# Two window-attention layers: 64x64 pieces of the TensorE array for the scores, windows taken in pairs with half of the heads each

## The chip, the cores and the metric

One core of a Trainium2 chip (trn2). The metric is the device time of the whole kernel in microseconds (us), from one launch. Everything is float32 where not said otherwise.

## What is computed

A batch of 16 images of 96 channels and 16x16 pixels goes through four residual layers, `x = x + layer(group_norm(x))`. Layers 0 and 1 are window attention: each image has four windows of 8x8 = 64 tokens, and 12 heads. Layer 2 is a quantized depthwise and pointwise convolution, layer 3 a spiking linear attention; the change does not touch them. Cut to what matters:

```python
# layer 0: head size 8, a bias per head, biases on q, k, v
qkv = xw @ qkv_w.T + qkv_b                       # xw: windows (64 tokens) x 96 channels
attn = einsum('bhnd,bhmd->bhnm', q * 8**-0.5, k) + rpb_table[rel_index]   # per head
out = softmax(attn) @ v ; out = out @ proj_w.T + proj_b
# layer 1: head size 32, image rolled by 4, one bias for all heads, masks in three of the four windows
dots = einsum('bhwid,bhwjd->bhwij', q, k) * 32**-0.5 + pos_emb[...] (+ UD_MASK, LR_MASK)
out = softmax(dots) @ v ; out = out @ w_out + b_out
```

## The kernel before

After some 120 us of loads and preparation the two attention layers run one after the other, each as 16 images ("samples"), software-pipelined by hand over five engines. Within a sample the unit of work is a *step*, four to a sample; before the change a step is one window with all 12 heads. Its scores lie in a tile `probs[w]` of 128 partitions (two heads x 64 queries) x 6 x 64 keys. Each step goes through this chain, and each engine runs its own queue strictly in the order written:

- PE, `pe_scores` (L749): six matmuls of 128x128x128 into one of the two banks `ps_scores[w % 2]`. The stationary operand is q of a window, masked so that of 128 columns each holds one head's 64 tokens (`q0` has 6 masked copies a sample, `q1` has 2 for each of 3 groups); the moving operand is k of the window and of the next (128 columns, of which the first 64 are wanted; the next group overwrites the rest). The zeros in k (rows of the other half `u`) and in q make the 128-deep contraction right. A bank is free once the vector engine has taken it (`biased`).
- DVE, `dve_scores`: add the bias from PSUM to `probs[w]` (L913) and row maximum (L916). POOL, `pool_shift` (L947): subtract it. ACT, `act_exp` (L804). DVE, `dve_sum` (L921, L923): row sum and reciprocal. POOL, `pool_scale` (L952).
- PE, `pe_transpose` (L757): three transposes into `ps_probsT`. ACT, `act_probsT` (L809): copy to SBUF. PE, `pe_values` (L770 in layer 1, L780 in layer 0): six matmuls with zero-padded v into `ps_heads`. ACT, `act_heads` (L814 four times a sample in layer 1, L817 once a sample in layer 0). Then per sample `pe_out` (L796, L798), `act_out` (L823) and `pool_residual` (L964).

Ahead of this, q, k and v of the next samples are made: DVE `dve_norm` (L938) writes the normalized image, PE `pe_qkv` (L720 for q and k, L728 for v) fills the two banks `ps_qkv` in turn, and each use of a bank is emptied by the engine that `qkv_plan` names, in so many instructions (`evac_q`, `evac_k`, `evac_v`: L836 or L842, L853 or L854, L866 or L873). PE may fill a bank again only when all of them are done.

The order is fixed by `pe_sample`, `act_sample`, `dve_sample` and `pool_sample`: in step w, DVE does the scores of w+2, then the sums of w+1, then the evacuations that `evacs_at[w]` lists; ACT does its evacuations first, then the exponential of w+2, then the copy of the transposes of w; PE, before the change, does half of the scores of w+3, the transposes of w, the other half, the values of w-1, then the q, k, v uses that `uses_at[w]` lists. So the scores of a step stand on PE more than a step ahead of the moment DVE wants them.

Of the kernel before, what the change touches and what calls it, by code (L numbers as in the profile page):

```python
# [25 lines left out]
ALU = mybir.AluOpType  # L26
# [4 lines left out]
T = SIDE * SIDE  # L31
# [13 lines left out]

CONSTS = {}
_at = 0
for _name, _n in (("ident", 128), ("qmask0", 6), ("qmask1", 2), ("group_mean", C), ("ones", 128),
                  ("head_blocks", C), ("masks", 4 * WT), ("rows", 2), ("minus_half", 1), ("perm", 4 * 128)):
    CONSTS[_name] = (_at, _at + _n)  # L50
    _at += _n
# [3 lines left out]
def constants():  # L55
# [10 lines left out]
    put("qmask0", (p[:, None] % 64 // HD0 == np.arange(NP * NH)) * np.float32(HD0 ** -0.5))  # L66
    put("qmask1", (p[:, None] // HD1 % 2 == np.arange(2)) * np.float32(HD1 ** -0.5))
# [7 lines left out]
    m = np.zeros((2, WT, NW, WT), bool)  # L75
    for w in range(NW):
        m[:, :, w] |= (ud & (w // 2 == 1)) | (lr & (w % 2 == 1))
    put("masks", m.reshape(128, NW * WT) * np.float32(NEG))


    perm = np.zeros((WT, NW, NH, WT))
    for w in range(NW):
        src = (tok // WIN + w // 2 * 4) % WIN * WIN + (tok % WIN + w % 2 * 4) % WIN
        perm[WT - 1 - src, w, :, tok] = 1
    put("perm", perm.reshape(WT, NW * 128), WT)
# [5 lines left out]
class Attention:  # L91


    def __init__(self, n, hd):
        self.n, self.hd = n, hd
        self.wide = hd == HD1
        self.slots = 2 if self.wide else NP * NH
# [8 lines left out]
        self.evacs_at = [[(1, 2, 0, 4)], [(1, 3, 0, 4)], [(1, 4, 0, 4)], [(2, 0, 0, 4), (2, 1, 0, 4)]] if self.wide else \  # L106
            [[(1, 0, 3, 6), (1, 1, 0, 2)], [], [(1, 2, 0, 4)], [(2, 0, 0, 3)]]


class AttentionSems:  # L110


    def __init__(self, sem, n):
# [5 lines left out]
        self.scores_ready = sem(f"l{n}_scores_ready")  # L119
        self.biased = sem(f"l{n}_biased")  # L120
# [15 lines left out]
def build(nc, a, out):  # L136

    ctx = ExitStack()
    with ctx:
# [30 lines left out]
        b0_q = sb("b0_q", [128, NP * NH])  # L170
        b0_v = sb("b0_v", [128, 2 * C])
# [8 lines left out]
        bias0 = sb("bias0", [128, NP * NU, WT])  # L180
# [5 lines left out]
        bias1 = sb("bias1", [128, NW, WT])  # L186
# [36 lines left out]
        q0 = [sb(f"q0_{i}", [128, NW, NP * NH, WT]) for i in range(2)]  # L223
        k0 = [sb(f"k0_{i}", [128, NU, T + WT]) for i in range(2)]

        v0 = [sb(f"v0_{i}", [128, NW * NP, NH, NH * NU * HD0]) for i in range(2)]
        q1 = [sb(f"q1_{i}", [128, 3, NW, 2, WT]) for i in range(2)]
        k1 = [sb(f"k1_{i}", [128, NU, NP, T + WT]) for i in range(2)]
        v1 = [sb(f"v1_{i}", [128, NW * NP, NH, NU * HD1]) for i in range(2)]
        probs = [sb(f"probs{i}", [128, NP * NU, WT]) for i in range(4)]  # L230
        row_max = [sb(f"row_max{i}", [128, NP * NU]) for i in range(4)]
        probsT = [sb(f"probsT{i}", [128, NP * 128]) for i in range(2)]
# [46 lines left out]
        def wait(eng, s, v):  # L279

            if not (isinstance(v, int) and v <= 0):
                eng.wait_ge(s, v)
# [59 lines left out]
        def first_loads():  # L342
# [8 lines left out]
            for k in range(2):  # L351
                yield b0_v[:, k * C:(k + 1) * C], a["L0_conv_qkv_b"][2 * C:3 * C].unsqueeze(0).broadcast_to([128, C])

            for h in range(NH):
                for u in range(NU):
                    yield (p0_raw[:, :].rearrange("o (p h u d) -> o h u p d", p=NP, h=NH, u=NU)[:, h, u],
                           a["L0_conv_proj_w"].rearrange("o (p u h d) -> o h u p d", p=NP, h=NH, u=NU)[:, h, u])
            yield p0_b[:, :], a["L0_conv_proj_b"].unsqueeze(1)

        def late_loads():  # L360
            yield w1[0:C, :], a["L1_conv_w_qkv"]

            for h in range(NH):
                for u in range(NU):
                    yield (p1[(h * NU + u) * HD1:(h * NU + u + 1) * HD1, :, :],
                           a["L1_conv_w_out"].rearrange("(p u h d) c -> h u d p c", p=NP, u=NU, h=NH)[h, u])
# [11 lines left out]
        def _(act):  # L378
# [4 lines left out]
            for dst, src in late_loads():  # L383
# [16 lines left out]
                        *(t[:, :, :] for t in k0),  # L400

# [1124 lines left out]
```

## Time and profile before

| | us |
|---|---|
| median of 3 runs | 680.67 |
| lowest, highest of them | 677.33, 831.42 |
| profiled execution: span from first to last instruction | 674.8 |
| median of the runs over that span | 5.9 |
| PE busy, DVE busy, ACT busy, POOL busy in the span | 522.9, 479.1, 319.7, 304.6 |

The span is that of one profiled execution; the time of a run also holds what lies around the first and the last instruction. Of the span, some 115 us are loads and preparation, about 190 us layer 0 (to 308 us), 250 us layer 1 (to 557 us) and 118 us layers 2 and 3. A matmul of float32 appears in the trace as two records (a transpose as one), so twelve records are six matmuls. The duration of a single record is longer than the distance between two, since they overlap; the chain of waits gives the distance.

### The profile page before, as it was taken

The page shows a single profiled execution, that of the slowest core. Times are in us where ns is not written, and L with a number is a line of the kernel's source. Part 1 is how long each engine was busy: PE and PEld are TensorE (multiplying, and loading weights), DVE is VectorE, ACT ScalarE, POOL GpSimd, SP SyncE. Part 2 cuts the span into 40 slices and gives each one's busy share as a digit, 9 for nine tenths or more (in the row PEclk, how much of TensorE's full clock was granted, in tenths as well). Part 3 has the DMA queues.
Part 4 walks back from the last instruction along what each step waited for, and adds up shares of the span by engine and source line. Part 5 has one row for each costly group of instructions (what it writes and reads, how often), then busy time and mean ns, then how long its engine had stood idle before and what let it go on. Part 6 is the DMA issues. An engine that isn't in the chain of part 4 may idle for free.

```text
span 674.8 us, 13829 instructions
## 1 busy us (share of the span) xinstructions
PE 522.9 (77%) x4459; PEld 420.9 (62%) x4459; DVE 479.1 (71%) x1237; ACT 319.7 (47%) x746; POOL 304.6 (45%) x482
## 2 busy tenths in 40 slices
PE   0000087689999999986999999999999998867664
PEld 0000086678888888874788888888888772323432
DVE  0000357699999999985788888788888748966784
ACT  0000000447575756644466666666666553226673
POOL 9000001267676666673365545555555553340322
PEclk9999999999999999999899999999999999987786
DMA  1111300000000000000000000000000000000001
GB/s 58 47 54 47 89 9 0 1 1 2 1 0 0 0 0 0 0 1 1 1 1 3 1 0 0 0 0 0 0 0 0 0 1 1 0 1 0 24 23 47
DMA packets 9808, 7.04 MB, mean 10 GB/s; under 512 B 6371, under 2 KB 9443, under 8 KB 9667
## 3 DMA queue, kind: packets, MB, share of 16 engines
q1 hardware_dynamic: 3954, 5.01, 2.4%
q10 hardware_dynamic: 5826, 1.67, 1.2%
q8 instruction: 15, 0.25, 0.2%
q14 instruction: 13, 0.11, 0.1%
HBM read 5.11 MB, written 1.57 MB: 10 GB/s over the span
## 4 chain that ended last, share of the span: by engine, by line
PE 49%; DVE 19%; SPq 11%; issue 7%; POOL 7%; ACT 4%; DVEq 1%; DMA 1%; POOLq 0%; ACTq 0%
PE bank L749 16%; SPq L327 11%; PE bank L720 9%; PE bank L757 5%; PE bank L770 4%; PE bank L796 3%; DVE conv L1172 3%; DVE probs L913 3%; DVE xn L938 3%; PE bank L728 3%; DVE row_max L916 3%; PE bank L1253 3%; POOL probs L952 3%; PE bank L557 2%; POOL probs L947 2%
## 5 line engine op out<-in xcount | busy, mean ns | idle before, releaser
L749 PE MATMUL bank<-k,q 128*128 128x128 f32 x1536 | 216.1, 278 | 8.2 <-issue 4.5
L749 PEld LDWEIGHTS bank<-k,q 128*128 128x128 f32 x1536 | 199.3, 193 | 22.7 <-issue 7.2
L947 POOL TENSOR_TENSOR probs<-probs,row_max 128x384 f32<-128x384 f32 x128 | 106.0, 828 | 181.2 <-DVE row_max L916 180.5
L804 ACT ACTIVATE probs<-probs 128x384 f32<-128x384 f32 x128 | 67.1, 524 | 115.1 <-POOL probs L947 113.9
L952 POOL TENSOR_TENSOR probs<-probs,inv_sum 128x384 f32<-128x384 f32 x128 | 106.1, 829 | 3.7 <-DVE inv_sum L923 3.7
L913 DVE TENSOR_TENSOR probs<-bank,bias 128x384 f32<-128x384 f32 x128 | 71.1, 555 | 35.8 <-PE bank L749 33.4
L916 DVE TENSOR_REDUCE row_max<-probs 128x6 f32<-128x384 f32 x128 | 70.8, 553 | 4.4
L539 PE MATMUL bank<-pos,cst 64*128 64x16 f32 x32 | 7.0, 371 | 86.1 <-DMA pos<-in_L_conv_pos_emb 86.1
L921 DVE TENSOR_REDUCE row_sum<-probs 128x6 f32<-128x384 f32 x128 | 69.5, 543 | 2.2 <-ACT probs L804 2.1
L757 PE MATMUL bank<-cst,probs 128*128 128x128 f32 x384 | 64.3, 276 | 7.2 <-POOL probs L952 5.6
L809 ACT COPY probsT<-bank 128x384 f32<-128x384 f32 x128 | 59.9, 468 | 2.9 <-PE bank L757 1.7
L842 ACT ACTIVATE q<-bank,b_q,cst 128x256 f32<-128x256 f32 x96 | 47.0, 564 | 29.4 <-PE bank L720 29.4
L539 PEld LDWEIGHTS bank<-pos,cst 64*128 64x128 f32 x32 | 6.9, 329 | 86.0 <-issue 86.0
L433 DVE CAST table_parts<-table 113x12 bf16<-113x12 f32 (+1 forms) x2 | 0.3, 175 | 78.1 <-DMA table<-in_L_conv_rpb_table 78.1
L720 PE MATMUL bank<-xn,w 128*128 128x256 f32 x192 | 51.5, 406 | 3.9 <-DVE v L866 3.2
L757 PEld LDWEIGHTS bank<-cst,probs 128*128 128x128 f32 x384 | 45.0, 141 | 12.3 <-POOL probs L952 12.1
L618 POOL TENSOR_SCALAR gn_veps<-gn_var 96x8 f32<-96x8 f32 x8 | 2.7, 340 | 104.2 <-DVE gn_var L612 104.2
L938 DVE TENSOR_SCALAR xn<-x,gn_mean,gn_rstd 96x32 f32 (+3 forms) x160 | 45.2, 347 | 0.1
L1454 ACT ACT_TABLE_LOAD x1 | 1.3, 1283 | 92.1 <-issue 92.1
L964 POOL TENSOR_TENSOR x<-y_attn,x 96x32 f32 (+3 forms) x160 | 42.5, 290 | 4.6 <-ACT y_attn L823 4.6
L720 PEld LDWEIGHTS bank<-xn,w 128*128 128x128 f32 x192 | 34.9, 195 | 11.1 <-issue 3.8
L836 ACT ACTIVATE q<-bank,cst 128x256 f32<-128x256 f32 x64 | 26.8, 470 | 23.9 <-PE bank L720 23.9
(144 smaller groups left out, 854.8 us busy)
## 6 DMA issues: line engine op xcount, KB each, us to landing
rel_bc<-in_L_conv_rel_index SPq DMA_DIRECT2D x1, 1808.0 KB
x<-in_x SPq DMA_DIRECT2D x4, 384.0 KB, 32.6
out_dram<-y_out SPq DMA_DIRECT2D x8, 192.0 KB, 2.1
cst<-in_consts ACTq DMA_DIRECT2D x1, 613.5 KB
w<-in_L_conv_w_qkv ACTq DMA_DIRECT2D x1, 432.0 KB, 3.9
p<-in_L_conv_w_out ACTq DMA_DIRECT2D x4, 36.0 KB, 3.3
b_qk<-in_L_conv_qkv_b ACTq DMA_DIRECT2D x8, 0.1 KB, 5.4
pos<-in_L_conv_pos_emb SPq DMA_DIRECT2D x8, 2.0 KB
```

The costliest lines, as they stand in the source:

```text
L327: sp.dma_start(x[:, i * n * T:(i + 1) * n * T].rearrange("c (b t) -> c b t", t=T), a["x"][i * n:(i + 1) * n].rearrange("b c h w -> c b (h ...
L720: last = nc.tensor.matmul(o[:, half * T:(half + 1) * T], w[:, col:col + 128], xn[par][:, :, :], start=True, stop=True)
L749: last = nc.tensor.matmul(ps_scores[w % 2][:, g * WT:(g + 2) * WT], q, k, start=True, stop=True)
L757: last = nc.tensor.transpose(ps_probsT[w % 2][:, p * 128:(p + 1) * 128], probs[w][:, 2 * p:2 * p + 2, :], ident)
L804: nc.scalar.activation(probs[w][:, :, :], probs[w][:, :, :], ACT.Exp).then_inc(L.s.exped, 1)
L809: nc.scalar.copy(probsT[w % 2][:, :], ps_probsT[w % 2][:, 0:NP * 128]).then_inc(L.s.probsT_sb, 1)
L913: nc.vector.tensor_tensor(probs[w][:, :, :], ps_scores[w % 2][:, 0:NP * NU * WT].rearrange("p (g k) -> p g k", k=WT), b, ALU.add).then_inc ...
L916: nc.vector.tensor_reduce(row_max[w][:, :], probs[w][:, :, :], AX.X, ALU.max).then_inc(L.s.maxed, 1)
L921: nc.vector.tensor_reduce(row_sum[w][:, :], probs[w][:, :, :], AX.X, ALU.add).then_inc(L.s.summed, 1)
L938: nc.vector.tensor_scalar(of_tokens(tokens), of_image(image(x_of(s))), gn_mean[:, bass.ds(s * 1, 1)], gn_rstd[:, bass.ds(s * 1, 1)], ALU.s ...
L947: nc.gpsimd.tensor_tensor(probs[w][:, :, :], probs[w][:, :, :], by_row(row_max[w]), ALU.subtract).then_inc(L.s.shifted, 1)
L952: nc.gpsimd.tensor_tensor(probs[w][:, :, :], probs[w][:, :, :], by_row(inv_sum[w]), ALU.mult).then_inc(L.s.scaled, 1)
```

## The change

A step is now a pair of windows (2j and 2j+1, index c) with half of the heads (index u), so there are still four steps a sample and each `probs[w]` still has 128 partitions (two windows x 64 queries) x 6 heads x 64 keys. The scores of both halves u of a pair are made by one call: twelve matmuls with a contraction of 64 rows (`rows = u*64..`), a stationary q of 64 columns and a moving k of 128 columns (two heads, of which each copy of k is masked to one). Rows u and output partitions c put each on one of four 64x64 quarters of the array, in the order p, c, u; half u goes to bank u. q is no longer masked by head (layer 1: one copy; layer 0: three copies, masked by group), k is, in two copies, by window. All evacuations of q and k are now ACT's. In layer 1 one copy of the heads serves a pair. The biases of v in layer 0 move to the copy of the heads. Lines of the new file: scores L749, transposes L758, values L771 and L783, exp L807, copy of the transposes L812, heads L817 (layer 1), q L838 or L844, k L857 or L861, v L881, norm L947, q and k matmuls L719, v matmuls L727, out L799 and L801.

Core of the diff:

```diff
-            return [("qk", 0, "act", 4), ("qk", 1, "dve", 4), ("qk", 2, "act", 4),
+            return [("qk", 0, "act", 3), ("qk", 1, "act", 3), ("qk", 2, "act", 3),
                     ("v", 0, "dve", 4), ("v", 1, "act", 4)]
-        return [("q", 0, "act", L.slots), ("k", 0, "dve", 2), ("v", 0, "dve", 4)]
+        return [("q", 0, "act", 3), ("k", 0, "act", 2), ("v", 0, "dve", 4)]
...
-        self.evacs_at = [[(1, 2, 0, 4)], [(1, 3, 0, 4)], [(1, 4, 0, 4)], [(2, 0, 0, 4), (2, 1, 0, 4)]] if self.wide else \
-            [[(1, 0, 3, 6), (1, 1, 0, 2)], [], [(1, 2, 0, 4)], [(2, 0, 0, 3)]]
+        self.evacs_at = [[(1, 2, 0, 3)], [(1, 3, 0, 4)], [(1, 4, 0, 4)], [(2, 0, 0, 3), (2, 1, 0, 3)]] if self.wide else \
+            [[(1, 1, 0, 2)], [], [(1, 2, 0, 4)], [(2, 0, 0, 3)]]
...
-    def pe_scores(pe, L, s, w, half):
-        if half == 0:
-            if w == 0:
-                for i in range(L.qk_uses):
-                    evacuated(pe, L, s, i)
-            wait(pe, L.s.biased, win_count(s, w - 2))
-        keys = slice(w * WT, (w + 2) * WT)
-        for g in range(half * NP, (half + 1) * NP):
-            p, u = g // NU, g % NU
-            if L.wide:
-                q, k = q1[par][:, p, w, :, :], k1[par][:, u, p, keys]
-            else:
-                q, k = q0[par][:, w, p * NH:(p + 1) * NH, :], k0[par][:, u, keys]
-            last = nc.tensor.matmul(ps_scores[w % 2][:, g * WT:(g + 2) * WT], q, k, start=True, stop=True)
+    def pe_scores(pe, L, s, j):
+        if j == 0:
+            for i in range(L.qk_uses):
+                evacuated(pe, L, s, i)
+        free = wait(pe, L.s.biased, win_count(s, 2 * j - 1))
+        for p in range(NP):
+            for c in range(2):
+                w = 2 * j + c
+                for u in range(NU):
+                    rows = slice(u * 64, (u + 1) * 64)
+                    q = (q1 if L.wide else q0)[par][rows, p, w * WT:(w + 1) * WT]
+                    k = k1[par][rows, p, w, :, :] if L.wide else k0[par][rows, w, :, :]
+                    one = nc.tensor.matmul(ps_scores[u][c * WT:(c + 1) * WT, p * 128:(p + 1) * 128], q, k,
+                                           start=True, stop=True)
+                    if p == NP - 1 and c == 1:
+                        one.then_inc(L.s.scores_ready, 1)
...
     def pe_sample(pe, L, s, prev, nxt, nxt2):
-        for w in range(NW):
-            ahead = w < 1 or nxt
-            if ahead:
-                pe_scores(pe, L, *at(s, w + 3), 0)
-            pe_transpose(pe, L, s, w)
-            if ahead:
-                pe_scores(pe, L, *at(s, w + 3), 1)
-            if w >= 1 or prev:
-                pe_values(pe, L, *at(s, w - 1))
-            if w == 1 and prev:
-                pe_out(pe, L, moved(s, -1))
-            q = uses(L, s, w, nxt, nxt2)
-            if q[2]:
-                pe_qkv(pe, L, *q)
+        for j in range(2):
+            if j == 0 or nxt:
+                pe_scores(pe, L, *pair_at(s, j + 1))
+            for u in range(NU):
+                w = 2 * j + u
+                pe_transpose(pe, L, s, w)
+                if u == 0 and (j or prev):
+                    pe_values(pe, L, *pair_at(s, j - 1))
+                q = uses(L, s, w, nxt, nxt2)
+                if q[2]:
+                    pe_qkv(pe, L, *q)
+            if j == 0 and prev:
+                pe_out(pe, L, moved(s, -1))
```

The values of a pair are twelve matmuls in one call (`pe_values(L, s, j)`, layer 0 in the order c, u, p, layer 1 in p, c, u), after the first transposes of the next pair. Evacuation of q and k, in short (q of layer 1 before: two masked copies; k before: once for each u and 64 rows, now once for each h and 128 rows, with the mask as scale):

```diff
-            src, dst = by_window(ps_qkv[b][:, 0:T]), q1[par][:, j, :, slot, :]
+            src, dst = ps_qkv[b][:, 0:T], q1[par][:, j, :]
-        rows = slice(u * 64, u * 64 + 64)
-        src = ps_qkv[b][rows, T:2 * T]
+        src = by_window(ps_qkv[b][:, T:2 * T])
+        scale = cst[:, lo:lo + 1]
```

In the preparation: the masked copies of k need no zeroed buffers; the constant table shrinks from 1227 to 842 columns; the position matmuls (L539, now L534) have 64 instead of 128 stationary columns and write windows 2j and 2j+1 to the two halves of the partitions; the bias of layer 0 is reduced once for 64 rows and then copied to the other 64 (one more DVE copy of 64x768); on ACT's DMA queue two broadcast loads of 128x96 become one of 96x1, four strided loads of `p0_raw` become one, and four of `p1` become one. On SP's queue nothing changes.

PE in layer 1, second half of a sample in the straight code ahead of the loop (steps 2 and 3). Before:

```order
L749 MATMUL bank<-k_0,q_0 128x128 x3
L757 MATMUL bank<-cst,probs 128x128 x3
L749 MATMUL bank<-k_0,q_0 128x128 x3
L770 MATMUL bank<-probsT,v_1 64x64 x6
L720 MATMUL bank<-xn,w 128x256 x4
L749 MATMUL bank<-k_0,q_0 128x128 x3
L757 MATMUL bank<-cst,probs 128x128 x3
L749 MATMUL bank<-k_0,q_0 128x128 x3
L770 MATMUL bank<-probsT,v_1 64x64 x6
L720 MATMUL bank<-xn,w 128x256 x2
```

The same half now (the first row holds the scores of the next sample's first pair; the scores of its second pair come after the last row):

```order
L749 MATMUL bank<-k_0,q_0 64x128 x12
L758 MATMUL bank<-cst,probs 128x128 x3
L771 MATMUL bank<-probsT,v_1 64x64 x12
L719 MATMUL bank<-xn,w 128x256 x4
L758 MATMUL bank<-cst,probs 128x128 x3
L719 MATMUL bank<-xn,w 128x256 x2
```

The scores that stood around every step's transposes now stand once a pair, ahead of them, and the two q and k matmuls of the third use come right before the next scores instead of after scores that DVE will want a step later.

ACT in layer 1, the same two steps. Before (evacuations of v; then of q and k of one use):

```order
L866 COPY v_0<-bank 64x6x32 x4
L804 ACTIVATE probs<-probs 128x384
L809 COPY probsT<-bank 128x384
L814 COPY heads_1<-bank 128x3x64
L836 ACTIVATE q_1<-bank,cst 128x4x64 x2
L853 COPY k_1<-bank 64x256 x2
L804 ACTIVATE probs<-probs 128x384
L809 COPY probsT<-bank 128x384
```

And now:

```order
L881 COPY v_0<-bank 64x6x32 x4
L807 ACTIVATE probs<-probs 128x384
L812 COPY probsT<-bank 128x384
L817 COPY heads_1<-bank 128x3x128
L838 ACTIVATE q_1<-bank 128x256
L857 ACTIVATE k_1<-bank,cst 128x4x64 x2
L838 ACTIVATE q_1<-bank 128x256
L857 ACTIVATE k_1<-bank,cst 128x4x64 x2
L807 ACTIVATE probs<-probs 128x384
L812 COPY probsT<-bank 128x384
```

The second use's q and k have come over from DVE and stand between the evacuation that PE waits for and the exponential that DVE waits for.

## Rows read from the trace of the kernel before

**Rows 1.** The page: busy time by engine, and the granted TensorE clock in 40 slices.

```profile
PE 522.9 (77%) x4459; PEld 420.9 (62%) x4459; DVE 479.1 (71%) x1237; ACT 319.7 (47%) x746; POOL 304.6 (45%) x482
...
PEclk9999999999999999999899999999999999987786
```

**Rows 2.** Windows: stretch, its length, busy by engine (instructions), clock, DMA share, GB/s.

```profile
115.00:120.00 5.00, 2.05 (x4) 1.18 (x4) 1.94 (x6) 2.56 (x6) 0.00 (x0) 1.00 0.01 2
...
170.00:210.00 40.00, 39.37 (x433) 34.66 (x431) 36.99 (x98) 24.86 (x57) 27.37 (x44) 1.00 0.00 0
...
395.00:435.00 40.00, 40.00 (x368) 34.98 (x368) 33.30 (x87) 26.02 (x68) 21.47 (x40) 1.00 0.00 0
```

**Rows 3.** Chain of waits in layer 1, 410 to 440 us: start, length, what.

```profile
by line: PE bank L749 35.7%; PE bank L720 22.0%; PE bank L770 15.0%; PE bank L728 9.9%; PE bank L796 9.8%; PE bank L757 8.7%
...
424.41 0.50 PE bank L770 x12
...
426.83 0.67 PE bank L749 x6
...
428.99 1.06 PE bank L720 x4
...
439.00 0.50 PE bank L770 x12
```

**Rows 4.** Timeline of DVE in layer 1: start, length, line, tiles, count.

```profile
428.67 0.56 DVE L913 TENSOR_TENSOR probs<-bank,bias 128x384 f32<-128x384 f32 x1
...
430.98 1.63 DVE L938 TENSOR_SCALAR xn<-x,gn_mean,gn_rstd 96x64 f32 x6
...
432.53 0.54 DVE L913 TENSOR_TENSOR probs<-bank,bias 128x384 f32<-128x384 f32 x1
...
435.86 0.56 DVE L913 TENSOR_TENSOR probs<-bank,bias 128x384 f32<-128x384 f32 x1
```

**Rows 5.** Timeline of the same stretch of layer 1, ACT and POOL.

```profile
430.09 0.84 ACT L836 ACTIVATE q<-bank,cst 128x256 f32<-128x256 f32 x2 [0.73 <-PE bank L720]
...
433.74 0.83 POOL L947 TENSOR_TENSOR probs<-probs,row_max 128x384 f32<-128x384 f32 x1 [2.23 <-DVE row_max L916]
...
434.60 0.52 ACT L804 ACTIVATE probs<-probs 128x384 f32<-128x384 f32 x1 [1.76 <-POOL probs L947]
...
435.03 0.46 ACT L809 COPY probsT<-bank 128x384 f32<-128x384 f32 x1
...
435.39 0.32 ACT L814 COPY heads<-bank 128x192 f32<-128x192 f32 x1
...
437.09 0.83 POOL L947 TENSOR_TENSOR probs<-probs,row_max 128x384 f32<-128x384 f32 x1 [1.74 <-DVE row_max L916]
```

**Rows 6.** Timeline of DVE in layer 0.

```profile
269.54 0.56 DVE L913 TENSOR_TENSOR probs<-bank,bias 128x384 f32<-128x384 f32 x1
...
271.36 0.56 DVE L913 TENSOR_TENSOR probs<-bank,bias 128x384 f32<-128x384 f32 x1
...
276.35 0.56 DVE L913 TENSOR_TENSOR probs<-bank,bias 128x384 f32<-128x384 f32 x1 [0.19 <-PE bank L749]
...
278.21 1.00 DVE L854 TENSOR_SCALAR k<-bank,b_qk 64x256 f32<-64x256 f32 x2
279.25 0.42 DVE L586 BATCH_NORM_STATS2 stats<-x  x1
...
280.58 0.56 DVE L913 TENSOR_TENSOR probs<-bank,bias 128x384 f32<-128x384 f32 x1
```

**Rows 7.** Chain of waits in layer 0: a step's values.

```profile
273.65 0.37 PE bank L780 x12
```

**Rows 8.** Chain of waits at the start of the kernel.

```profile
78.56 7.37 DMA pos<-in_L_conv_pos_emb
...
86.07 6.98 PE bank L539 x32
...
120.33 2.94 PE bank L749 x12
```

More of the change, by code:

```diff
@@ L361, in late_loads @@
             yield w1[0:C, :], a["L1_conv_w_qkv"]
[L363 to L366, printed above, removed]
+            yield p1[:, :, :], a["L1_conv_w_out"].rearrange("(p r) c -> r p c", p=NP)
             yield p1_b[:, :], a["L1_conv_b_out"].unsqueeze(1)
@@ L473, in bias_banks @@
                     n = min(BIAS_KEYS, WT - k0_)
-                    for h in range(NH):
-                        src = bank[2 + i][0:WT, 0:n * 3 * HEADS] \
-                            .rearrange("q (k part g h) -> q h g k part", k=n, part=3, h=NH)[:, h]
-                        step(nc.vector.tensor_reduce(bias0[h * WT:(h + 1) * WT, :, k0_:k0_ + n], src, AX.X, ALU.add))
+                    src = bank[2 + i][0:WT, 0:n * 3 * HEADS].rearrange("q (k part g) -> q g k part", k=n, part=3)
+                    step(nc.vector.tensor_reduce(bias0[0:WT, :, k0_:k0_ + n], src, AX.X, ALU.add))
             bias_banks(0, 2)
@@ L768, in pe_values @@
                 for p in range(NP):
-                    for h in range(NH):
-                        last = nc.tensor.matmul(ps_heads[h * WT:(h + 1) * WT, p * WT:(p + 1) * WT],
-                                                v1[parity(s)][:, w * NP + p, h, :], pT[:, p * 128 + h * WT:p * 128 + (h + 1) * WT],
-                                                start=True, stop=True)
+                    for c in range(2):
+                        for u in range(NU):
+                            last = nc.tensor.matmul(ps_heads[u * WT:(u + 1) * WT, p * 128 + c * WT:p * 128 + (c + 1) * WT],
+                                                    v1[par][:, 2 * j + c, p * NU + u, :],
+                                                    probsT[2 * j + u][:, p * 128 + c * WT:p * 128 + (c + 1) * WT],
+                                                    start=True, stop=True)
@@ new lines, in evac_v @@
+                dst = v1[par][rows, 2 * j + c, :, h * HD1:(h + 1) * HD1]
+            else:
+                src = ps_qkv[b][src_rows, 0:2 * C].rearrange("k (g u h d) -> k h g u d", u=NU, h=NH, d=HD0)[:, h]
+                n = 2 * NP
+                lo = h * HD0
+                step = NU * NU * NH * HD0
+                dst = v0[par][rows, c * n:(c + 1) * n, :, :].rearrange("k g u e -> k g (u e)")
+                dst = bass.AP(tensor=dst.tensor, offset=dst.offset + lo,
+                              ap=[dst.ap[0], [step, n], [NU * NH * HD0 + NH * HD0, NU], [1, HD0]])
@@ L875, in evacuate @@
+            return nc.scalar.copy(dst, src) if eng == "act" else nc.vector.tensor_copy(dst, src)
         def evacuate(eng, who, L, s, i, first=0, end=99):
```

195 lines of the change are left out of this document (97 added, 98 removed).

## Prediction, made before the changed kernel had run

> **What bounds the kernel now.** I read the page first. No engine is busy over 77% of the span [rows 1], but that is a mean over stages, so I read the windows of the two attention layers next. In layer 1 PE is busy 40.00 us of 40, in layer 0 39.37, and DVE 36.99 [rows 2]. Then the chain of waits. In layer 1 it stands on PE alone, 35.7% of it on the scores (L749), and one sample is 439.00 - 424.41 = 14.59 us [rows 3]. Eight groups of six score records at 0.67 are 5.36 us of these: 0.111 us a record of 128 columns. Last the timelines. In layer 0 a sample is 280.58 - 269.54 = 11.04 us [rows 6], and DVE idles only 0.19 us in it ahead of a step that waited for scores. So layer 1 is PE's, and layer 0 is DVE's with PE close behind. The loads and the preparation are a chain of their own [rows 8]; layers 2 and 3 don't change.
>
> **The scores.** There are as many score records as before, 48 a sample, but each uses a quarter of the array. What 24 of them (one pair) take, call it D, decides much. No row shows a matmul on half of the rows. From above: one after the other at 0.111 is D = 2.67. From below: four at a time without loss is 0.67. The nearest rows are the values, which already use a part of the columns each: twelve records in 0.50 us in layer 1 [rows 3], 0.042 each with the changes of shape around them, and twelve in 0.37 in layer 0 [rows 7], 0.031 each. Such records are of 64 columns and would take about 0.055 alone, so pieces of the array do work side by side, and 0.031 to 0.042 looks like what a record costs at least. 24 x 0.031 to 24 x 0.042 is 0.74 to 1.0; I take D = 0.9. The change of shape between matmuls is in the 0.042. The Trainium skill (TensorEngine Tiling, Array Packing, Key Properties) says that changing the tiling mode drains the engine, which would speak against more kinds of shapes in one queue. But the values changed it already, four times in and out a sample; now values and scores do so twice each, and the count is the same. The skill (TensorE: Matmul & The Clock Gate, Part 3, Packing small matmuls) gives tiles that run together the time of one plus 4 ns for each further one; by that three groups of four would be 3 x 0.235 = 0.70, an estimate from its rule, and the result some 3 us lower.
>
> **Layer 0.** DVE loses the two evacuations of k: 278.21 to 279.25, 1.04 us [rows 6]. The evacuations of v stay four, and all else on DVE keeps its size. ACT has 5 evacuations of 128x256 in place of 6 and 24.86 us of 40 busy [rows 2], so it covers k. Without k and the wait of 0.19 the sample is 9.81. What is late next? The scores of a pair may start when the second of the pair before has been taken: 0.56 us into its step. DVE wants them one step later, 271.36 - 269.54 = 1.82. 0.56 + 0.9 and two hops of 0.05 are 1.56: they fit, by 0.26. Once a sample PE comes to them a little late, after the out matmul, for which I put 0.1. So 9.9, a gain of 1.1, 14 times: 15.4 us.
>
> **Layer 1.** By sums it looks splendid: PE 14.59 - 5.36 + 1.8 = 11.0, DVE about 10.9 (two steps of 1.82 and the two stretches of the next sentences), ACT under 10. But the order closes a loop. PE does the third q/k use at the end of a sample; it needs the bank that ACT empties in step 3, and behind this use in PE's queue stand the scores that DVE wants at once. Before, those had been made in the step ahead. Once around: ACT empties the first use, 3 at 0.84/2 [rows 5] = 1.26; PE the third use 1.06 [rows 3]; scores 0.9; DVE step 0 with statistics and the norm, 428.67 to 432.53 = 3.86; step 1 with v, to 435.86 = 3.33 [rows 4]; from the start of step 2 to POOL's shift, 437.09 - 435.86 = 1.23; from shift to exponential 434.60 - 433.74 = 0.86; exponential, copy of the transposes and heads on ACT 0.43 + 0.36 + 0.36 [rows 5], and ACT is at the first use again. With two hops 13.75 us. That is the new period, with no engine busy over 80% of it. The gain is 0.84 x 14 = 11.8 us. It is bounded by 0 and by 14 x 3.5 = 49 (if the loop didn't close, DVE's 10.9 and some hops). If D grows, this loop grows by the same.
>
> **Ends of the layers.** In the last two samples of each layer no q, k, v are made; a step was PE's: 1.33 + 0.33 (three transposes at 0.111) and 0.37 or 0.50, so 2.04 and 2.17, and is DVE's 1.82 now. 8 x 0.22 + 8 x 0.35 is 4.6; I take 4.
>
> **Start.** PE's position matmuls stand on the chain with 6.98 us for 32 records [rows 8], 0.22 each, twice what a record of 128 stationary columns takes in the loops [rows 3]. With 64 columns I take half: 3.4 us less (0 to 3.5), since what follows waits for them. The position data land last on SP's queue, whose own loads don't change; the constants are 30% smaller and seven DMAs fewer go through the other queue beside it. That shares the engines that move them, so the position data may land earlier: I take 2 us (0 to 8, the latter a tenth of the 86). The one reduction less for each bias bank pays for the copy of the bias. The first scores took 2.94 us for twelve records [rows 8], at half pace; DVE can start a pair sooner, and the second window of it at once. ACT's last evacuation ahead of it comes some 0.4 sooner in layer 0 and a little later in layer 1. Together 4 us for both layers.
>
> **The sum.** 15.4 + 11.8 + 4 + 3.4 + 2 + 4 = 40.6 us. The span of 674.8 becomes 634.2. The median of the runs lay 5.9 above that span, which gives 640.
>
> **Rivals.** (1) *The quarters don't run side by side.* For: only pieces of columns are shown to do so, and here all need weights of their own. D = 2.67. In layer 0 DVE then waits at each second step, 0.56 + 2.67 + 0.1 - 1.82 = 1.51, twice a sample: 9.81 + 3.02 = 12.8, 1.8 more than before, 25 us. Layer 1: 13.75 + 1.77 = 15.5, 13 us more. Ends: 7 more; start 6 less. 680.7 + 39 = 720 us, slower. It decides from D = 1.9 on; below that the change wins. (2) *Only two at a time*, D = 1.33: layer 0 waits 0.17 twice, gains 0.9 (12 us), layer 1 0.41 (6), ends 3, start 8: 652 us. (3) *The clock.* PE falls from 98% busy in layer 0 to about 70%, and in the last four slices of the kernel the granted clock is 0.6 to 0.8 [rows 1]. Against: in a stretch with 2.05 of 5 us busy it was 1.00 [rows 2], and the gaps here are under a microsecond. At 1.2 in place of 2.4 GHz for half of the time, layer 1's loop would gain back 1.0 of its 0.84, layer 0's scores about 1 us a sample: about 670 us, no change that a measurement of this kernel can tell. (4) *Layer 1's loop doesn't close*, because ACT gets to the first use sooner than I have it, or PE's third use is ready earlier: each microsecond is 14. With half of it gone 620, with all of it 603 us.
>
> **How the numbers follow.** The forecast (632 to 648) has 0.58, rival 2 0.15, rival 4 to 622 and below 0.09, rival 3 and other small losses that leave nothing 0.11, rival 1 0.07. I count 2% (13.6 us) as what a measurement of this kernel can tell from no change. Faster: 0.58 + 0.15 + 0.09 and a little of the third, 0.84. Same 0.09, slower 0.07. The range takes in the forecast, the upper half of rival 4 and rival 2 with a clock or wait that costs 10 us more: 620 to 664.
>
> **What would show it.** The changed profile should have 24 score records of a pair (L749) in about 0.9 us; a layer 0 sample of 9.9 us with DVE nearly full; a layer 1 sample of 13.75 us in which DVE idles once a sample, ahead of step 0, for about 2.9 us with PE named, while PE itself idles ahead of L719 for ACT's k. The position matmuls should take 3.5 us. Score groups of 1.3 us or more, DVE waits ahead of every second step in layer 0, or a granted clock under 1 in the loops would prove it wrong; so would a layer 1 sample under 13 us with no wait of DVE for PE.

## The result, and the profile after

The changed kernel takes 655.54 us (median of 4 runs, 654.75 to 656.62) against 679.00 for the kernel before in the same session (4 runs, 675.88 to 831.42). The ratio is 0.969, with a 95% interval of 0.965 to 0.973: 3% faster. The run of 831.42 was a slow one, and the ratio compares fast runs alone. The forecast was 640 with a range of 620 to 664: the sign and the range hold, and of the gain of 40 us little more than half came, 23.5. The profiled span went from 674.8 to 653.0.

The page of the changed kernel, busy time and the granted clock:

```profile
PE 411.4 (63%) x4459; PEld 270.3 (41%) x4459; DVE 444.5 (68%) x1138; ACT 305.2 (47%) x714; POOL 299.2 (46%) x478
...
PEclk9999999959999999976899999999999989977786
```

PE lost 111.5 us of work [rows 1]; the records of L749 alone fell from 216.1 to 61.1 us. No engine is over 68% now. And the line of the clock has two dents that the one of before lacks: a 5 about 140 us in, the first samples of layer 0, and 7, 6, 8 about 290 us in, the end of layer 0. Stretches of the changed kernel, as in [rows 2]: the first samples of layer 0, its loop, its end, and the loop of layer 1:

```profile
130.00:170.00 40.00, 28.92 (x396) 19.95 (x389) 34.70 (x93) 21.90 (x50) 26.86 (x41) 0.79 0.01 2
...
210.00:250.00 40.00, 27.10 (x471) 18.61 (x469) 37.06 (x97) 25.34 (x58) 28.69 (x47) 1.00 0.00 0
...
280.00:285.00 5.00, 2.25 (x13) 1.55 (x17) 2.66 (x7) 2.15 (x5) 4.19 (x6) 0.82 0.00 0
...
290.00:295.00 5.00, 3.89 (x53) 2.95 (x54) 4.39 (x11) 2.12 (x5) 3.85 (x7) 0.50 0.00 2
295.00:300.00 5.00, 4.16 (x38) 2.49 (x39) 3.29 (x10) 2.25 (x6) 3.47 (x7) 0.50 0.02 5
...
390.00:430.00 40.00, 32.48 (x369) 22.30 (x370) 29.57 (x78) 26.36 (x72) 22.78 (x42) 1.00 0.00 0
```

Before, the stretch from 130 to 170 us ran at full clock:

```profile
130.00:170.00 40.00, 36.08 (x383) 31.63 (x382) 36.77 (x99) 22.80 (x52) 25.25 (x37) 1.00 0.01 2
```

Layer 0's loop is still DVE's (37.06 of 40). In layer 1 nothing is full. To see where the 21.8 us of span come from I took the start of each sample's norm (`xn`, L938 before, L947 after) from the timeline of DVE, sample 0 to 15 of either layer:

| stretch, from norm to norm | before | after | gain | forecast |
|---|---|---|---|---|
| start to the first norm | 115.00 | 111.20 | 3.8 | 5.4 |
| layer 0, samples 0 to 4 | 42.76 | 42.01 | 0.7 | 5.3 |
| layer 0, samples 4 to 15 (11 a layer) | 121.83 (11.08 each) | 114.59 (10.42) | 7.2 | 12.1 |
| end of layer 0, to layer 1's first norm | 26.56 | 29.25 | -2.7 | 2.0 |
| layer 1, samples 0 to 4 | 51.86 | 52.04 | -0.2 | 4.5 |
| layer 1, samples 4 to 15 | 160.53 (14.59) | 151.83 (13.80) | 8.7 | 9.2 |
| from there to the end | 156.26 | 152.08 | 4.2 | 2.0 |

The last column shares the forecast's terms out over these stretches: its "14 times" a layer as 11 in the loop and 3 in the first samples, its 4 us for the ends and 4 for the first pairs in halves. So layer 1 came as foreseen, and the shortfall lies in layer 0, in its end, and in the first samples of both layers.

One caution on these lengths. The traces of e3, e7 and e9 below have the same code as the changed kernel in all samples of layer 0 but the last two, and e3 in those too. There samples 0 to 4 took 40.97, 42.93 and 42.91, a sample of the loop 10.52, 10.53 and 10.41, and e3's end of layer 0 took 28.02 in place of 29.25. So 1 to 2 us in a stretch, or 0.1 in a sample, can differ between two executions of the same code.

The chain of waits in layer 1, from one "third use" of PE to the next (start, length, what):

```profile
413.75 1.13 PE bank L719 x4
414.88 0.89 PE bank L749 x24
415.76 0.55 DVE probs L923
...
419.68 0.47 DVE probs L923
...
422.94 0.57 DVE probs L923
...
424.17 0.84 POOL probs L956
...
425.95 0.48 ACT heads L817
426.44 0.29 ACT q L838
426.73 0.73 ACT k L857 x2
427.51 1.13 PE bank L719 x4
428.64 0.89 PE bank L749 x24
```

This is the loop of the forecast, link by link: third use, scores, DVE's steps 0 and 1 and the start of step 2, POOL's shift, ACT's heads and first evacuation, third use again. 427.51 - 413.75 = 13.76 us. In [rows 3] the chain of the same stretch was PE alone. Twenty-four score records take 0.89: in the trace they start in six groups of four, 0.007 apart within a group and 0.11 to 0.16 from group to group, the last 0.60 behind the first, and a record then runs for 0.27. DVE starts 0.88 behind the first.

DVE and POOL in layer 0, about one norm (timeline, then the durations of that norm's four instructions, shortest, median and longest in ns):

```profile
225.75 0.42 DVE L581 BATCH_NORM_STATS2 stats<-x  x1
226.10 1.57 DVE L947 TENSOR_SCALAR xn<-x,gn_mean,gn_rstd 96x64 f32 x4
226.12 0.82 POOL L961 TENSOR_TENSOR probs<-probs,inv_sum 128x384 f32<-128x384 f32 x1
227.00 0.55 PE L758 MATMUL bank<-cst,probs 128*128 128x128 f32 x3 [1.00 <-POOL probs L961]
...
L947 DVE TENSOR_SCALAR xn<-x,gn_mean,gn_rstd x4: 301/302/899, 226.1 to 227.4; 96x64 f32 x4
```

Before, the same norm took 0.97 (four instructions of 0.30, 0.22 apart). Now it is 1.57 and 1.24 in turn. Where it is 1.57 the first of the four took 899 ns in place of 302; it began while POOL was still at its shift, and POOL's scale followed at once and kept its 0.82. Where it is 1.24 the first took 566. In both it ends 0.05 us after POOL's scale (227.00 after 226.95, 216.59 after 216.54). This was not in my sum, and a row had it: in [rows 4] the six instructions of layer 1's norm take 1.63 and not 1.4, since one of them took 0.58 and ended 0.05 after POOL's. Nor was the end of layer 0. PE's timeline there:

```profile
277.57 0.31 PE L626 MATMUL bank<-gn_in,cst 96*96 96x16 f32 x2 [2.58 <-DVE gn_in L602]
...
282.75 0.56 PE L758 MATMUL bank<-cst,probs 128*128 128x128 f32 x3 [2.99 <-POOL probs L961]
...
290.08 1.56 PE L749 MATMUL bank<-k,q 64*64 64x128 f32 x24
292.27 0.90 PE L758 MATMUL bank<-cst,probs 128*128 128x128 f32 x3 [0.63 <-POOL probs L961]
...
300.92 4.41 PE L719 MATMUL bank<-xn,w 128*128 128x256 f32 x12
```

In the group norm PE stands idle for 2.58 and 2.99 us. Before, the longest gap there was 1.61, since score matmuls filled the rest. Behind these gaps the granted clock is at the lower level, 1.2 GHz, from 283 to 287 and from 290 to 304 us (0.50 in two of the windows above): L749 x24 takes 1.56 in place of 0.89, the transposes 0.90 in place of 0.55.

### The profile page after: what moved, and what is told of

It is laid out like the page before. It is cut to its first block, busy times and chain, and to the rows that moved or that the text cites. A ratio compares the mean times of both kernels' runs of the same rounds, so it can differ in the third digit from the quotient of the medians.

```text
span 653.0 us, 13734 instructions
## 1 busy us (share of the span) xinstructions
PE 411.4 (63%) x4459; PEld 270.3 (41%) x4459; DVE 444.5 (68%) x1138; ACT 305.2 (47%) x714; POOL 299.2 (46%) x478
## 3 DMA queue, kind: packets, MB, share of 16 engines
HBM read 4.82 MB, written 1.57 MB: 10 GB/s over the span
## 4 chain that ended last, share of the span: by engine, by line
DVE 33%; PE 22%; SPq 12%; issue 11%; POOL 11%; ACT 7%; DVEq 1%; DMA 1%; ACTq 0%; POOLq 0%
SPq L332 11%; DVE probs L923 7%; DVE row_max L925 6%; PE bank L749 5%; DVE v L881 5%; POOL probs L956 5%; PE bank L719 4%; DVE row_sum L930 3%; DVE conv L1180 3%; DVE xn L947 3%; POOL probs L961 3%; PE bank L1261 3%; PE bank L552 2%; PE bank L758 2%; ACT k L857 2%
## 5 line engine op out<-in xcount | busy, mean ns | idle before, releaser
L807 ACT ACTIVATE probs<-probs 128x384 f32<-128x384 f32 x128 | 67.7, 529 | 157.5 <-POOL probs L956 157.5
L758 PE MATMUL bank<-cst,probs 128*128 128x128 f32 x384 | 74.1, 305 | 80.5 <-POOL probs L961 71.9
L758 PEld LDWEIGHTS bank<-cst,probs 128*128 128x128 f32 x384 | 42.3, 147 | 119.7 <-POOL probs L961 106.2
L719 PE MATMUL bank<-xn,w 128*128 128x256 f32 x192 | 52.7, 414 | 20.1 <-ACT k L857 15.7
L749 PE MATMUL bank<-k,q 64*64 64x128 f32 x1536 | 61.1, 293 | 3.1 <-ACT k L861 1.8
L812 ACT COPY probsT<-bank 128x384 f32<-128x384 f32 x128 | 60.5, 472 | 2.2 <-PE bank L758 1.8
L534 PE MATMUL bank<-pos,cst 64*64 64x16 f32 x32 | 2.4, 266 | 86.9 <-DMA pos<-in_L_conv_pos_emb 86.9
L749 PEld LDWEIGHTS bank<-k,q 64*64 64x64 f32 x1536 | 44.6, 141 | 25.1 <-issue 23.7
L947 DVE TENSOR_SCALAR xn<-x,gn_mean,gn_rstd 96x32 f32 (+3 forms) x160 | 51.6, 386 | 0.0
L719 PEld LDWEIGHTS bank<-xn,w 128*128 128x128 f32 x192 | 36.0, 200 | 29.8 <-ACT k L857 19.6
L857 ACT ACTIVATE k<-bank,cst 128x256 f32<-128x256 f32 x96 | 42.1, 516 | 0.0
L881 DVE COPY v<-bank 64x96 f32<-64x96 f32 (+1 forms) x128 | 38.9, 304 | 3.1
L534 PEld LDWEIGHTS bank<-pos,cst 64*64 64x64 f32 x32 | 2.3, 217 | 86.8 <-issue 86.8
```

The lines of the kernel that those rows point to most:

```text
L719: last = nc.tensor.matmul(o[:, half * T:(half + 1) * T], w[:, col:col + 128], xn[par][:, :, :], start=True, stop=True)
L749: one = nc.tensor.matmul(ps_scores[u][c * WT:(c + 1) * WT, p * 128:(p + 1) * 128], q, k, start=True, stop=True)
L758: last = nc.tensor.transpose(ps_probsT[w % 2][:, p * 128:(p + 1) * 128], probs[w][:, 2 * p:2 * p + 2, :], ident)
L807: nc.scalar.activation(probs[w][:, :, :], probs[w][:, :, :], ACT.Exp).then_inc(L.s.exped, 1)
L881: return nc.scalar.copy(dst, src) if eng == "act" else nc.vector.tensor_copy(dst, src)
L947: nc.vector.tensor_scalar(of_tokens(tokens), of_image(image(x_of(s))), gn_mean[:, bass.ds(s * 1, 1)], gn_rstd[:, bass.ds(s * 1, 1)], ALU.s ...
```

## Experiments

Twelve kernels, three sets of four, each set on one chip beside its own runs of the kernel before (677.36, 676.60 and 674.73 us there). Times are medians of 4 runs (10 for e4). "Sample" is the mean over samples 4 to 15 of a layer, as in the table, in one trace. The changed kernel was not run again in these sets, and the runs of the kernel before differ by up to 2.6 us between them, so a difference of 3 us or less to its 655.54 is not clear of noise unless the kernels compared are of one set.

**e1: k back on DVE in layer 0.**

```diff
-            return [("q", 0, "act", 3), ("k", 0, "act", 2), ("v", 0, "dve", 4)]
+            return [("q", 0, "act", 3), ("k", 0, "dve", 2), ("v", 0, "dve", 4)]
```

> The changed kernel with one part undone: layer 0's two evacuations of k go back to DVE (1.04 us a sample). Theory A (DVE's norm takes 1.24 to 1.57 us in the changed kernel in place of 0.97 because, with k gone from DVE, it falls on POOL's scale): with k in between the norm is clear of POOL again and takes 0.97, the sample is 10.44 + 1.04 - 0.44 = 11.0 us, +0.6 a sample, some 8 us more than the changed kernel (664). Rival B (the norm is longer for another reason, POOL has no part in it): norm stays at 1.24 to 1.57, sample 11.5 us, 14 to 15 us more (670).

662.91 us (661.78 to 663.15). DVE's timeline of it:

```profile
218.73 1.00 DVE L862 TENSOR_SCALAR k<-bank,cst,b_k 128x256 f32<-128x256 f32 x2
219.64 0.41 DVE L581 BATCH_NORM_STATS2 stats<-x  x1
219.98 0.97 DVE L947 TENSOR_SCALAR xn<-x,gn_mean,gn_rstd 96x64 f32 x4
```

POOL's scale ran from 218.91 to 219.74 there, beside k (which reads PSUM, and took its 1.00) and clear of the norm, which is back at 0.97. The sample is 10.87, and the whole 7.4 us more than the changed kernel. Theory A: of the 1.04 us that k leaves on DVE, 0.44 come back as a longer norm.

**e2: the norm one instruction later.** Layer 0's norm moves behind the bias-add of step 1.

```diff
             nc.vector.tensor_tensor(out, scores, b, ALU.add).then_inc(L.s.biased, 1)
+            if between:            # layer 0, step 1: dve_norm(dve, L, moved(s, 2)), no longer ahead of dve_scores
+                between()
```

> The changed kernel with DVE's norm of layer 0 moved by one instruction in step 1: between the bias-add and the maximum in place of ahead of the bias-add. POOL's scale of the step before is over by then, and its next work waits for the maximum. Theory A (norm and POOL's scale share something): L947 x4 takes 0.97 us each time, a sample of layer 0 goes from 10.44 to 9.9 to 10.1 us, 5 to 7 us less in all (649). Rival B: norm stays at 1.24 to 1.57 us and the time is the same within 2 us.

654.32 us (652.50 to 657.69), sample 10.37. A miss, and an instructive one. The norm did fall, to 0.97 and 1.12 (of the latter its first instruction still met the end of POOL's scale: it ended at 226.74, POOL at 226.69). But DVE then idled ahead of its scores:

```profile
218.73 0.56 DVE L923 TENSOR_TENSOR probs<-bank,bias 128x384 f32<-128x384 f32 x1 [0.36 <-PE bank L749]
...
226.29 1.12 DVE L949 TENSOR_SCALAR xn<-x,gn_mean,gn_rstd 96x64 f32 x4
...
229.10 0.56 DVE L923 TENSOR_TENSOR probs<-bank,bias 128x384 f32<-128x384 f32 x1 [0.54 <-PE bank L749]
```

The scores set layer 0 as well, and the long norm had only covered that. In the changed kernel they stand in PE's queue behind transposes that wait 1.0 to 1.25 us for POOL's scale.

**e3: layer 1's scores ahead of the third use.** In `pe_sample`, for layer 1:

```diff
+                    if early and w == 3 and nxt:         # early: layer 1; at j == 0 only for sample 0
+                        pe_scores(pe, L, moved(s, 1), 1)
                     q = uses(L, s, w, nxt, nxt2)
                     if q[2]:
                         pe_qkv(pe, L, *q)
```

> The changed kernel with PE's order altered in layer 1 alone: the scores of the next sample's second pair stand ahead of the third q/k use and not behind it. Theory A (layer 1's sample of 13.84 us is a loop through ACT's first evacuation, PE's third use and these scores): DVE's wait of 3.0 us ahead of its step 0 goes, the sample falls to 12.0 to 12.8 us, 14 samples make 15 to 25 us less (630 to 640). Rival B (DVE waits for something that these scores need anyway, or ACT or POOL is the bound): the wait moves to another step and the sample stays over 13.5 us, the time within 4 us of 655.5.

636.31 us (635.73 to 637.90), sample 12.00 in place of 13.80: theory A. What DVE waited for in the loops of layer 1 (total us, times, longest), first in the changed kernel, then in e3:

```profile
DVE probs L923 <- PE bank L749: 35.6, 12, 3.1
```

```profile
DVE probs L923 <- PE bank L749: 8.6, 12, 0.9
DVE row_sum L930 <- ACT probs L807: 5.4, 12, 0.5
```

One line in another place gives 19 us, nearly as much as the whole change.

**e4: the same quarter in a row.**

```diff
-            for p in range(NP):
-                for c in range(2):
-                    for u in range(NU):
+            for c in range(2):
+                for u in range(NU):
+                    for p in range(NP):
```

> The changed kernel with its 24 score records of a pair in another order: three in a row on the same quarter of the array, in place of neighbours on different quarters; nothing else changes. Theory A (neighbours run side by side only if they stand on different quarters): of each three, two pay 0.111 us for themselves, D is 8 x 0.222 to 8 x 0.25 = 1.8 to 2.0 us in place of 0.89; layer 1's loop grows by 0.9 to 1.1 a sample to some 14.9 us, layer 0 by 0.6 to 1.4, the time by 25 to 35 us to 680 to 690. Rival B (the records cost their issue alone, in any order): D stays 0.9 and the time is the same.

684.45 us (676.77 to 689.36): within 2% of the kernel before, and if anything slower, ratio 1.009 (1.005 to 1.012). PE's timeline, in the trace of the slowest of its runs:

```profile
427.34 1.69 PE L749 MATMUL bank<-k,q 64*64 64x128 f32 x24
```

The text on record took records for matmuls: a float32 matmul is two records, so this order puts six records on a quarter in a row, and the order of the change two. The 24 records take 1.69 here. Their starts show how: they fall into four trains of six, a quarter each by the order of the program, with 0.16 and then 0.11 from record to record, and each train starts 0.275 behind the one before. In the changed kernel the four trains have the same steps but start 0.007 apart. (Which record belongs to which train is read from the spacing; the records that signal DVE stand at the ends of the third and the fourth train, as they should.) So the pace on one quarter is the same in either order, 0.11 a record as before on the whole array, and the order decides how soon the other quarters join: 0.825 + 0.60 + 0.27 = 1.69 against 0.02 + 0.60 + 0.27 = 0.89. Theory A, with D smaller than I put it. Layer 0's sample is 11.77, at a mean clock of 0.91 and 0.96 over 170 to 210 and 210 to 250 us. Layer 1's is 14.31, only 0.51 longer though D grew by 0.80: bank 0 is ready three matmuls before the end here and one before, and DVE starts on bank 0. That this is the whole reason was not tried.

**e5, e6: layer 0's scores sooner**, right behind the transposes of windows 1 and 3; e6 has the norm of e2 too.

```diff
                     pe_transpose(pe, L, s, w)
+                    if u and behind[j] and nxt:          # behind: layer 0; at j == 0 ahead only for sample 0
+                        pe_scores(pe, L, moved(s, 1), j)
```

> The changed kernel with PE's order altered in layer 0 alone: the scores of the next pair stand right behind the transposes of windows 1 and 3, ahead of the v use, the out matmul and the k use; DVE's norm stays where it is. Theory A (DVE's waits for L749 in layer 0, 0.40 us in every second sample, come from what stands ahead of the scores in PE's queue): the waits go, a sample is DVE's own work with its norm at 1.24 to 1.57, 10.2 us in place of 10.44, 2 to 4 us less in all (652). Rival B (the scores then wait for DVE's bias-add behind the norm and hold up the v use and the out matmul behind them): waits of DVE grow elsewhere, the sample stays at 10.4 to 10.8 and the time is 655 to 660.

> Both edits of layer 0 at once: the norm between bias-add and maximum (as in e2, where it fell to 0.97 to 1.12 us but DVE then waited 0.36 to 0.54 for scores four times in two samples) and the scores right behind the transposes. Theory A (in the changed kernel two things hold layer 0, the norm beside POOL's scale and the scores' place in PE's queue, and either alone uncovers the other): the sample falls to 9.85 to 10.05 us, 14 samples make 5 to 8 us less, 648 to 650. Rival B (POOL's scale and the transposes behind it set the step, wherever norm and scores stand): sample 10.3 to 10.4, time 653 to 655.

e5: 655.98 us (653.30 to 659.08), no gain; its sample is 10.63, longer than the 10.42 of the changed kernel and in the range of its rival B. e6: 650.58 (650.44 to 651.01), 5.0 less than the changed kernel: two things did hold layer 0, and only both edits together show a gain. But e6's sample is 10.29 and not 9.95, and the windows 210 to 250 name a third thing, the clock, 0.83 in either. e6's:

```profile
210.00:250.00 40.00, 32.35 (x452) 23.07 (x445) 34.84 (x97) 24.69 (x57) 28.99 (x46) 0.83 0.00 0
```

PE and DVE in e6 (timeline), about one of these falls:

```profile
224.10 0.90 PE L758 MATMUL bank<-cst,probs 128*128 128x128 f32 x3 [1.00 <-POOL probs L963]
224.94 1.56 PE L749 MATMUL bank<-k,q 64*64 64x128 f32 x24
...
226.63 0.56 DVE L923 TENSOR_TENSOR probs<-bank,bias 128x384 f32<-128x384 f32 x1 [0.72 <-PE bank L749]
```

The scores took 1.56 in place of 0.89, and DVE waited 0.72 for them.

**e7, e9: idle work at the end of layer 0.** PE multiplies constants into an empty bank of `ps_qkv` where it stood idle.

```diff
+            for _ in range(n):     # e7: 8 ahead of the group norm, 8 and then 2 a step; e9: 2, 5 and 3
+                nc.tensor.matmul(ps_qkv[b][:, 0:T], ident, cst[:, 0:T], start=True, stop=True)
```

> The changed kernel with idle work for PE at the end of layer 0: 8 matmuls of 256 columns (0.23 us each) ahead of the group norm's matmul, 8 in the first step of sample 14, 2 in each of the seven steps behind it, into a bank that nobody reads. Theory A (the granted clock falls to 0.50 between 290 and 303 us because PE stood idle for 2.58 and 2.99 us in the group norm, and this makes L749, L758, L783 and L719 there take up to twice as long): the clock stays near 1.00, L719 x12 takes 3.1 in place of 4.41 us, and layer 1's first scores come 3 to 6 us sooner, 650 to 652 in all. Rival B (the chain through the group norm, POOL's scale and DVE sets this stretch, PE's pace doesn't matter): the clock is up and the time the same within 1.5 us, or longer by the 0.5 us a step that the idle work takes.

> The changed kernel with idle work for PE only where it stood idle at the end of layer 0: 2 matmuls (0.46 us each, as two records of 0.23) ahead of the group norm's matmul, 5 behind the values of sample 14's first step, 3 behind those of its third; 4.6 us in all, where e7 had 14. Theory A (e7 brought the clock to 1.00 but its idle work stood in the way of scores and transposes, which ate the gain): the clock stays at 0.95 or more from 275 to 305 us, nothing is held up by more than 0.5 us, and norm starts of layer 1's first sample come 2 to 4 us sooner than in the changed kernel (297.05): 651 to 653. Rival B (the end of layer 0 is set by the group norm on DVE and POOL and the steps behind it, PE's pace is hidden): clock up, time within 1.5 us of 655.5.

e7: 658.22 us (656.29 to 658.58), 2.7 more. The clock was 1.00 from 270 to 310 us, but a matmul is two records of 0.23, so that the idle work was twice what I had put, 3.69 us ahead of the group norm's matmul alone, and stood in the way. e9: 652.75 us (652.30 to 654.09), 2.8 less than the changed kernel; by the ratios to the kernel before, 0.967 (0.962 to 0.971) against 0.969 (0.965 to 0.973), neither e7 nor e9 is clear of no change. In e9's trace the end of layer 0 takes 27.10 in place of 29.25, at a mean clock of 0.91 from 280 to 300:

```profile
280.00:300.00 20.00, 15.91 (x218) 11.12 (x217) 14.45 (x38) 8.24 (x19) 14.56 (x24) 0.91 0.01 2
```

Against e3's 28.02, the same code as the changed kernel with a clock of 0.67 there, it is 0.9. The cleanest pair is e10 and e11 below, from one chip: the same idle work takes 1.6 us off the time and 1.2 off this end. So the clock costs 1 to 2 us there and not 5. What sets the rest of this end was not tried; In e7, with the clock at 1.00 and its idle work in the way, it took 30.58.

**e8, e10 to e12: together.** e10 is e6 with the scores right behind the transposes in layer 1 too; e8 adds e7's idle work to it, e11 e9's; e12 is e11 and one idle matmul a sample in layer 0's loop, ahead of window 1's transposes.

```diff
+                    if not L.wide and w == 1 and nxt2:   # after a wait until the bank is empty
+                        nc.tensor.matmul(ps_qkv[b][:, 0:T], ident, cst[:, 0:T], start=True, stop=True)
                     pe_transpose(pe, L, s, w)
```

> e3, e6 and e7 in one kernel, and in layer 1 the scores stand right behind the transposes of windows 1 and 3. If the four causes are separate their gains add: 636.3 of e3, less 5 to 8 for layer 0, less 3 to 5 for the clock: 624 to 628 us. Rival B (the losses cover each other, as PE is the bound of layer 1 at 36.6 of 40 us and more waits take the place of those removed): 632 to 636.

> e8 (628.7 us) without its idle work: the norm behind the bias-add in layer 0, scores right behind the transposes of windows 1 and 3 in both layers. Theory A (e8's idle work cost 2 to 3 us as in e7): 625 to 627. Rival B (in e8, with less slack elsewhere, the higher clock paid for it): 629 to 632.

> e10 with e9's smaller idle work at the end of layer 0. If e9's theory A holds, 2 to 4 us less than e10: 622 to 625. If its rival holds, the same as e10 within 1.5 us.

> e11 and in layer 0's loop one idle matmul (0.46 us) a sample ahead of window 1's transposes, where PE stood idle for 1.00 us. Theory A (with the scores sooner, PE's gaps let the granted clock fall inside layer 0's loop, 0.83 over 210 to 250 us in e6, where L749 x24 took 1.56 in place of 0.89 us and DVE waited 0.72 for it; less idle time keeps it up): clock 0.95 or more in 160 to 270 us, a sample 9.85 to 10.0 in place of 10.2, 2 to 4 us less than e11. Rival B (the falls have nothing to do with this gap): clock in the loop still 0.85 to 0.95, time the same or 1 to 3 us more.

| | median us (runs) | layer 0 sample | end of layer 0 | layer 1 sample | clock 210 to 250 |
|---|---|---|---|---|---|
| e8 | 628.74 (627.96 to 630.13) | 10.31 | 27.61 | 12.01 | 0.91 |
| e10 | 626.60 (626.28 to 627.88) | 10.14 | 26.46 | 11.99 | 0.91 |
| e11 | 624.96 (623.66 to 626.28) | 10.05 | 25.21 | 12.00 | 0.91 |
| e12 | 621.84 (621.45 to 622.62) | 9.91 | 25.20 | 11.99 | 1.00 |

The parts add, and more than in full: e3's 19.2 and e6's 5.0 off the 655.54 would give 631.3, and e10 has 626.60; where the other 4.7 come from was not tried, and they are measured across sets. e11 against e10 is 1.6, less than the 2 to 4 of its text, and their runs touch. e12 against e11 is 3.1, of one set, and their runs do not touch. It supports that idle time of PE lets the clock fall inside the loop: with 0.46 us of useless work a sample in a gap of 1.00 us it is 1.00 in place of 0.91, and the sample comes to the 9.9 that I had forecast. The mean clock of the whole kernel is 0.955 to 0.958 in e12's four runs and 0.936 to 0.947 in e11's. The longest gap alone does not tell: between 210 and 250 us PE's longest gap is 1.25 in the changed kernel, at a clock of 1.00, and 1.04 in e6, at 0.83. e12's windows 210 to 250:

```profile
210.00:250.00 40.00, 31.92 (x480) 20.45 (x480) 37.09 (x102) 26.83 (x62) 30.50 (x50) 1.00 0.00 0
```

Its ratio to the kernel before is 0.920 (0.916 to 0.924): 52.9 us, over twice what the change alone brings.

## Why the prediction was right, and what it had wrong

- **The scores (D = 0.9).** Right: 0.89, partly by luck. I took a price per record from the values, 0.031 to 0.042. The starts of the records give another sum: four at a time at the old pace of 0.11, 0.67 for the 24 as in my bound from below, and some 0.2 until the last ones are through. Rival 2 (D = 1.33) fell with it, and so did rival 1, but e4 shows how near rival 1 lies: the same 24 records in another order take 1.69, and lose all of the gain; I had put the point where the change stops winning at D = 1.9. The Trainium skill (TensorE: Matmul & The Clock Gate, Part 3) would have given 0.70, an estimate from its rule; the trace has 0.89 from the first start to the last end, and decides.
- **Layer 1 (13.75).** Right: 13.80. The chain of the changed kernel walks the loop as it was drawn, and e3, which cuts the loop at the link that the forecast named, takes 1.8 us a sample out. Rival 4, the loop that doesn't close, didn't come by itself; e3 makes it come, and what it then gives is about half of the 3.5 us a sample that I had as its bound, where PE is at 36.6 of 40 us; what sets the 12.00 was not tried.
- **Layer 0 (9.9).** Wrong, 10.42, in two steps. The first is "all else on DVE keeps its size". The removed k had stood beside POOL's scale, and with it gone the norm stands there: 0.27 and 0.60 us more in turn, 0.44 in the mean (e1, e2). The second is "the scores of a pair may start when the second of the pair before has been taken". They may, but PE's queue is strict, and ahead of them stood transposes that waited for POOL; before, [rows 2] had PE at 39.37 of 40, and such waits were hardly seen. That is DVE's wait of 0.40 in every second sample; e2 and e5, which each mend one of the two, gain nothing clear, and e6, which mends both, does. 9.81 + 0.44 + 0.20 = 10.45. Half of the gain of 1.1 a sample went there.
- **"14 times".** Wrong: only 11 samples a layer run at the loop's pace. The first four of both layers gained 0.7 and -0.2 us, where the forecast had 9.8 with the first pairs. In layer 0 the first two samples gained 2.1 us, and the next two lost 1.4 (13.50 and 12.75 us, 12.91 and 11.99 before). These two are the stretch in which the granted clock was 0.50, from 130 to 147 us; before it was 1.00 there. That is rival 3 again. How much of the 4.6 missing it explains stays open: e3, the same code with the lower clock for 3.4 us in place of 17, took 1.0 less than the changed kernel for the four samples, but e7 and e9, with 10.2 us of it, took 0.9 more.

  In both kernels layer 1 starts with PE idle until DVE has emptied a bank of v, and then with the second sample's q and k, mostly at 1.2 GHz, before and after:

```profile
321.58 4.63 PE L720 MATMUL bank<-xn,w 128*128 128x256 f32 x12 [3.21 <-DVE v L866]
```

```profile
313.36 4.51 PE L719 MATMUL bank<-xn,w 128*128 128x256 f32 x12 [4.37 <-DVE v L881]
```

  PE's idle time there is 1.2 us longer than before. How the rest of these first samples splits was not tried; in e1, e2, e5, e6, e7 and e9, with the same code in layer 1, they took 50.4 to 53.6 us.
- **Ends of the layers (4).** Mis-sized in layer 0, and with the wrong sign: 2.7 us were lost. Part of this is rival 3, the clock, in a place where I had not looked for it: I had weighed the loops, "the gaps here are under a microsecond", and not the group norm, in which PE's score matmuls had been the filling. e9 and e11 put the clock's part at 1 to 2 us. But e9's end, at 27.10, still takes 0.5 more than the 26.56 of before, where 2.0 less was forecast, and its own idle work is in that; this part is open. Layer 1's end gained, with the last two samples, 4.2.
- **Start (3.4 + 2).** The position matmuls fell from 6.98 to 2.36, 4.6 less, more than half. The DMA gave nothing: the matmuls could start at 86.86, 0.8 later than before (86.07), though fewer bytes moved beside it. The first norm came 3.8 sooner.
- **The clock in the loops** was 1.00 as forecast from 170 to 250 us and from 390 to 430 in the changed kernel's trace. But it was near: e3, with the same layer 0, has one fall of 3.4 us in that loop (0.96 from 210 to 250), and in e5 and e6, with the gaps placed a little otherwise, it falls to 0.83.
- **The total.** The measured 655.54 lies nearer to rival 2's 652 than to the 640. That is chance: rival 2's D of 1.33 is not in the trace.

## What to carry to other kernels

When an instruction is taken off an engine, look at what then falls into its place beside the other engines, not only at the engine's own sum. A gain is worth the number of times that the loop really runs at its own pace; the ends and the first turns need a sum of their own, and an engine that has become free may lose its clock there. And after a change that relieves the bound engine, read its in-order queue again: here moving one call of the scores gave nearly as much as the rewrite.

## What the runs showed of the hardware that was not expected

- An instruction of the norm on DVE (96x64, float32, SBUF to SBUF) takes 302 ns, and one took 899 while POOL worked on SBUF beside it; POOL keeps its 0.82 us. Evacuations out of PSUM beside the same POOL instruction (k, 1.00 for two, in e1) show none of it. The Trainium skill (SBUF — State Buffer, "SBUF: two separate sides") says that the two engines share one pair of ports, which the first to come locks for its whole instruction while the other blocks; on DVE's side this holds for instructions in a two-port mode or with two inputs in SBUF, and no run shows in which mode the norm runs. The trace agrees with the lock: wherever the norm meets POOL's scale in layer 0's loop, its instruction ends 0.05 us after POOL's.
- Matmuls on different 64x64 quarters run at the same time, each quarter at 0.11 us a record of 128 columns, and the order in the queue decides when a quarter joins: 0.89 or 1.69 us for the same 24 records.
- The granted clock fell to 0.50 for over 10 us behind two gaps of PE of 2.6 and 3.0 us, and its mean to 0.83 over 40 us of a loop whose longest gap was 1.04 us (e6), while a loop with gaps of 1.25 us kept 1.00. With 0.46 us of useless work a sample it was 1.00 (e12), without it 0.91 (e11).
